# Layer 1 of a recommendation model: embeddings stationary and 512 columns of W1 moving in seven of eight blocks, the sums turned at a block's end

## The chip, the cores and the metric

One core of one Trainium2 chip. The metric is the device time of one execution in microseconds (us), the median of several. TensorE (PE) multiplies, its weight loads are listed apart as PEld; ScalarE (ACT) and VectorE (DVE) move and transform; GpSimd (POOL) issues the gathers; SyncE (SP) issues plain transfers.

## The reference, cut to what matters

```python
B, F_CAT, F_CONT, V, D = 2048, 26, 13, 12500, 64        # batch, features, vocabulary, width
H1, H2 = 1024, 512
first = sum(cat_t1[f, cat[:, f]]) + sum(cont_t1 * cont)
E = concat([cat_t2[f, cat[:, f]], cont_t2 * cont], axis=1)          # 2048 x 39 x 64
s = sum(E, axis=1);  fm_second = 0.5 * sum(s * s - sum(E * E, axis=1), axis=1)
h = relu(batchnorm(E.reshape(2048, 2496) @ W1 + b1, g1, be1))       # statistics over the batch
h = relu(batchnorm(h @ W2 + b2, g2, be2))
out = sigmoid(bias + first + fm_second + (h @ W3 + b3)[:, 0])       # returned as [1 - out, out]
```

## The kernel before, in words

The batch of 2048 is 16 tiles of 128 rows, taken two at a time in 8 blocks of 256 rows (BT = 2, BC = 256). The 26 categorical features are 13 pairs k = 0..12 (KT = 13). A pair is one 128-row slice of W1's first 1664 rows.

**Gathers.** POOL fetches each pair of each block with 4 indirect DMAs (2 tiles by 2 features, L255), 416 in all. Ahead of a pair's four it waits for `transposed`, `summed`, `squared` and `idx_ready` (L246 to L249). The first lets it run at most three pairs ahead of TensorE's transposes (five in the first block): the gather of pair k of a block waits until pair k - 3 is transposed. DVE makes the indices at the start (`find_rows`, L459) and copies those of the next block into `idx_now` pair by pair (`stage_indices`).

**Layer 1 in a block.** TensorE turns a pair (`transpose`, L735: two 128x128 transposes into one of three PSUM buffers), ACT copies it to `x_sb` (L286), and TensorE multiplies it two pairs later (LEAD = 2) with all of W1's 1024 channels: 8 products (L744), in each of which a 128x128 piece of W1 is stationary and the block's 256 rows of `x_sb` move. The trace has two records for each such fp32 product. The sums have the channels on the partitions and the batch along the columns. The continuous features add one product of 14 rows per channel chunk at the block's head (`continuous`, L787). The 8 chunks of sums fill 4 PSUM banks. `HELD` says which two chunks go into a bank: (0, 7), (1, 2), (3, 4), (5, 6).

**A block's end** (`finish`). TensorE finishes bank after bank with the last two pairs. After the second bank it does the next block's small products (`misc_products`) and transposes its pair 0, after the fourth its pair 1 (NEXT_AT). ACT copies each bank to `h1` (`sums_out`, L299), squares and copies the next block's pairs 0 and 1 in between, and DVE takes the batch statistics from `h1` (L528). `continuous` of the next block waits for `acc_free` of each bank.

**The last block** (b = 7) stands outside the loop. There the products catch up: two pairs are multiplied behind the transpose of pair 3, two behind that of pair 7, and from then on each pair is multiplied behind its own transpose. DVE takes the statistics straight from PSUM (`last_stats`, L598), makes scale and shift of layer 1 in five parts (`norm1`), ACT makes `hhi` and `hfull` (L362, L370), DVE `hlo` (L613), and layer 2 (L819) runs through to the end.

Each engine works through its list in program order. There is no scheduler. The order is the one in which the code is written.

## Time and profile before

| | us |
|---|---|
| time, median of 3 runs (lowest, highest) | 632.85 (632.6, 633.41) |
| the profiled execution, its own time | 632.65 |
| its span, first to last instruction | 630.9 |
| PE busy | 558.8 |
| PEld busy | 447.9 |
| POOL busy | 393.5 |
| ACT busy | 212.4 |
| DVE busy | 148.7 |
| mean granted clock of TensorE | 0.981 of 2.4 GHz |

The busy times are of the span. TensorE's records overlap, since matmuls are pipelined and their ends are modelled: the distance from start to start says more than a record's length. A row of the timeline merges like instructions that follow one another and gives their number.

### The profile page before, as it was taken

What the parts mean: (1) busy time and instruction counts of PE and PEld (TensorE: products, weight loads), DVE (VectorE), ACT (ScalarE), POOL (GpSimd) and SP (SyncE); (2) the same over time, 40 slices, a digit from 0 to 9 for tenths busy, and PEclk for the clock granted to TensorE, in tenths of its full rate; (3) what the DMA queues carried; (4) which work ended last, traced back from release to release, by engine and by line L of the source; (5) the groups of instructions that cost most, each with busy time, mean ns of one, the idle gap of its engine ahead of it and who ended that gap; (6) DMA issues with size and microseconds to landing.
All of it is one profiled execution on the core that took longest, in us unless ns stands there. A gap on an engine that the chain in (4) does not pass through costs nothing.

```text
span 630.9 us, 8473 instructions
## 1 busy us (share of the span) xinstructions
PE 558.8 (89%) x2534; PEld 447.9 (71%) x2534; DVE 148.7 (24%) x465; ACT 212.4 (34%) x682; POOL 393.5 (62%) x423
## 2 busy tenths in 40 slices
PE   6999898789778977799779978998799999999998
PEld 1588786568666866687658766776678877888886
DVE  1111130013001201130013101311122204754365
ACT  1223132223222322232223222322223414998575
POOL 5777777777777777777777777777777771000000
PEclk9789999999999999998999899989998999999999
DMA  8953333334332333234323432374233331000000
GB/s 256 346 137 28 27 27 27 27 26 27 27 28 25 28 27 27 27 26 28 27 26 27 28 26 27 27 161 26 27 27 28 28 27 10 1 2 0 1 0 2
DMA packets 18139, 26.79 MB, mean 42 GB/s; under 512 B 7699, under 2 KB 7947, under 8 KB 18124
## 3 DMA queue, kind: packets, MB, share of 16 engines
q0 software_dynamic: 13312, 13.87, 28.1%
q1 hardware_dynamic: 4496, 12.66, 5.7%
q8 instruction: 8, 0.13, 0.1%
q10 hardware_dynamic: 316, 0.07, 0.1%
q14 instruction: 7, 0.06, 0.0%
HBM read 26.56 MB, written 0.02 MB: 42 GB/s over the span
## 4 chain that ended last, share of the span: by engine, by line
PE 45%; DMA 31%; issue 12%; POOL 5%; ACT 2%; DVE 2%; POOLq 1%; ACTq 0%; DVEq 0%; SPq 0%
DMA emb<-in_table,idx_now 31%; PE bank L744 20%; PE bank L819 14%; POOL emb L255 5%; PE bank L787 4%; PE bank L718 2%; PE bank L735 2%; ACT junk L293 2%; DVE idx_now L477 1%; PE bank L777 1%; DMA h<-in_w 1%; DVE bank L494 0%; PE bank L778 0%; ACT h L421 0%; POOLq L137 0%
## 5 line engine op out<-in xcount | busy, mean ns | idle before, releaser
L255 POOL DMA_INDIRECT emb<-in_table,idx_now x416 | 392.8, 944 | 129.7 <-issue 115.7
L744 PE MATMUL bank<-x_sb,w_sb 128*128 128x256 f32 x1664 | 384.3, 386 | 2.4 <-ACT x_sb L286 2.4
L744 PEld LDWEIGHTS bank<-x_sb,w_sb 128*128 128x128 f32 x1664 | 314.7, 194 | 44.3 <-ACT x_sb L286 3.6
L293 ACT ACTIVATE junk<-emb 128x128 bf16<-128x128 f32 x208 | 64.2, 309 | 253.3 <-DMA emb<-in_table,idx_now 241.0
L494 DVE TENSOR_TENSOR bank<-emb,bank 128x260 f32<-128x260 f32 x91 | 39.3, 432 | 318.8 <-DMA emb<-in_table,idx_now 318.8
L735 PE MATMUL bank<-ident,emb 128*128 128x128 f32 x208 | 43.9, 294 | 59.1 <-DMA emb<-in_table,idx_now 58.2
L735 PEld LDWEIGHTS bank<-ident,emb 128*128 128x128 f32 x208 | 23.2, 141 | 88.4 <-DMA emb<-in_table,idx_now 80.2
L286 ACT ACTIVATE x_sb<-bank 128x256 f32<-128x256 f32 x104 | 38.3, 369 | 65.4 <-PE bank L735 65.3
L819 PE MATMUL bank<-hhi,w2hi 128*128 128x512 f32 x128 | 50.8, 397 | 0.0
L819 PE MATMUL bank<-hhi,w2lo 128*128 128x512 f32 x128 | 50.4, 394 | 0.0
L819 PE MATMUL bank<-hlo,w2hi 128*128 128x512 f32 x128 | 39.0, 396 | 0.3 <-DVE hlo L613 0.3
L293 ACT ACTIVATION_READ_ACCUMULATOR junk<-emb (+1 forms) x208 | 38.9, 187 | 0.0
L299 ACT ACTIVATE h<-bank 128x512 f32 (+1 forms) x32 | 19.0, 595 | 56.3 <-PE bank L744 56.3
L528 DVE BATCH_NORM_STATS2 stats<-h x56 | 21.1, 419 | 56.7 <-ACT h L299 56.7
L787 PE MATMUL bank<-cont_sb,m_sb 14*128 14x256 f32 x128 | 32.5, 407 | 0.0
L362 ACT ACTIVATE hhi<-h,bn 128x512 fp32r<-128x512 f32 x32 | 25.9, 809 | 10.0 <-PE bank L819 7.8
L613 DVE TENSOR_TENSOR hlo<-hfull,hhi 128x512 fp32r<-128x512 f32 x32 | 22.1, 690 | 30.4 <-ACT hfull L370 30.4
L787 PEld LDWEIGHTS bank<-cont_sb,m_sb 14*128 14x128 f32 x128 | 24.8, 198 | 5.5 <-issue 1.3
L819 PEld LDWEIGHTS bank<-hlo,w2hi 128*128 128x128 f32 x128 | 23.9, 187 | 6.5 <-DVE hlo L613 0.7
L819 PEld LDWEIGHTS bank<-hhi,w2hi 128*128 128x128 f32 x128 | 24.0, 187 | 6.2 <-issue 0.3
L819 PEld LDWEIGHTS bank<-hhi,w2lo 128*128 128x128 f32 x128 | 24.0, 187 | 5.7
L370 ACT ACTIVATE hfull<-h,bn 128x512 f32<-128x512 f32 x32 | 25.7, 803 | 0.0
(83 smaller groups left out, 171.6 us busy)
## 6 DMA issues: line engine op xcount, KB each, us to landing
emb<-in_table,idx_now POOLq DMA_INDIRECT x416, 3.3
w_sb<-in_w SPq DMA_DIRECT2D x13, 512.0 KB, 19.4
h<-in_w SPq DMA_DIRECT2D x6, 512.0 KB, 7.2
w2raw<-in_w SPq DMA_DIRECT2D x8, 256.0 KB, 5.4
h<-in_w SPq DMA_DIRECT2D x1, 256.0 KB, 12.7
idx_all<-in_cat SPq DMA_DIRECT2D x1, 182.0 KB, 2.5
cont_sb<-in_cont_t SPq DMA_DIRECT2D x8, 13.0 KB
diag<-in_cont_diag ACTq DMA_DIRECT2D x1, 45.5 KB, 2.1
```

What stands on the lines that cost most here:

```text
L255: nc.gpsimd.indirect_dma_start(out=emb[:, j, at:at + ROW], out_offset=None, in_=table, in_offset=bass.IndirectOffsetOnAxis(ap=idx_now[:, j ...
L286: nc.scalar.activation(x_sb[:, k, :], tp[k % TP], ACT.Copy).then_inc(x_ready, 1)
L293: nc.scalar.activation(junk[:, :], emb[:, j, k * PAIR + 1:k * PAIR + 1 + P], ACT.Square, accum_out=esq[:, ds(b * BT + j, 1), k]).then_inc( ...
L362: nc.scalar.activation(hhi[:, k, :], src, ACT.Relu, bias=bn1[:, SHIFT, k:k + 1], scale=bn1[:, SCALE, k:k + 1]).then_inc(h_high, 1)
L370: nc.scalar.activation(hfull[:, i % 2, :], h1[:, k, n * NB2:(n + 1) * NB2], ACT.Relu, bias=bn1[:, SHIFT, k:k + 1], scale=bn1[:, SCALE, k:k ...
L494: nc.vector.tensor_tensor(tot, rows, tot, ALU.add).then_inc(summed, 1)
L528: nc.vector.bn_stats(stats1[:, c, ds(b, 1), :].rearrange("p b s -> p (b s)"), h1[:, c, ds(b * BC, BC)]).then_inc(stats1_done, 1)
L613: nc.vector.tensor_tensor(hlo[:, k, :], hfull[:, i % 2, :], hhi[:, k, :].bitcast(f32), ALU.subtract).then_inc(h_split, 1)
L735: done = nc.tensor.transpose(tp[s][:, j * P:(j + 1) * P], emb[:, j, k * PAIR + 1:k * PAIR + 1 + P], ident[:, :])
L744: return nc.tensor.matmul(acc[c], w1_sb[:, k, c * P:(c + 1) * P], x_sb[:, k, :], start=False, stop=stop, skip_group_check=True)
L787: done = nc.tensor.matmul(acc[c], m_sb[:, c * P:(c + 1) * P], cont_sb[:, :], start=(c == HELD[m][0]), stop=False, skip_group_check=True)
L819: done = nc.tensor.matmul(bank2(n, m), w[:, k, cols], x[:, k, :], start=(k == 0 and i == 0), stop=(k == C1 - 1 and i == 2))
```

## The change

In blocks 0 to 6 the operands of layer 1 change places. A 128-column tile of `x_sb` (128 rows of the batch) is stationary, and 512 channels of W1 move (`tile_products`): 4 products per pair in place of 8, each into a whole bank. `sums` lists the banks as (half of the channels, tile): (0,0), (0,1), (1,0), (1,1). `continuous_tiles` is changed in the same way. The sums now have the batch on the partitions. So at a block's end ACT copies each bank to a scratch part of `h1`, the columns of the last block (`stage`); TensorE turns them with 16 transposes of 128x128 back into the four banks (`turn`); and ACT copies the banks out as before (`sums_out`), after all of the staging. Block 7 keeps its products, with chunks 2m and 2m + 1 in bank m. `HELD`, `LAST_AT` and a wait ahead of the last product go, and `last_stats` and `last_sums_out` follow the new banks. At the start DVE writes the first block's indices into `idx_all` and copies them to `idx_now` pair by pair. In the gather's waits `idx_ready` moves ahead of `summed`.

The diff, cut to its core:

```diff
@@ -136,7 +136,9 @@
     with ExitStack() as ctx:
         bank = [ctx.enter_context(nc.psum_tensor(f"bank{i}", [P, 512], f32)) for i in range(8)]
-        acc = [bank[q // 2][:, q % 2 * BC:q % 2 * BC + BC] for q in (0, *range(2, C1), 1)]
+        acc = [bank[c * BC // 512][:, c * BC % 512:c * BC % 512 + BC] for c in range(C1)]
+        HALF = H1 // 2
+        sums = [(half, j) for half in range(H1 // HALF) for j in range(BT)]
         tp = [bank[ACC_BANKS + i][:, 0:BC] for i in range(TP)]
         z = bank[4][0:TILES, 0:P]
         misc = bank[ACC_BANKS][:, BC:BC + BT * 128].rearrange("p (j c) -> p j c", j=BT)
...
@@ -196,10 +198,6 @@
         def bank2(n, m):
             return bank[(n + 1) % 2 * C2 + m][:, :]
-
-        HELD = [(0, C1 - 1)] + [(2 * m - 1, 2 * m) for m in range(1, ACC_BANKS)]
-
-        LAST_AT = [0, 1, 1, 2, 2, 3, 3, 4]
         W2_AT = {k: k - LEAD for k in range(LEAD, C1 + LEAD)}
...
@@ -244,9 +242,9 @@
                 for k in range(KT):
                     pool.wait_ge(transposed, b * KT + (KT + k + 1 - ahead))
+                    pool.wait_ge(idx_ready, b * KT + (k + 1))
                     pool.wait_ge(summed, b * KT + (k + 1))
                     pool.wait_ge(squared, b * (BT * KT) + BT * (k + 1))
-                    pool.wait_ge(idx_ready, b * KT + (k + 1))
                     pool.sem_inc(slot_open, 1)
                     for j in range(BT):
                         for half in range(2):
...
@@ -293,22 +291,26 @@
                     nc.scalar.activation(junk[:, :], emb[:, j, k * PAIR + 1:k * PAIR + 1 + P], ACT.Square,
                                          accum_out=esq[:, ds(b * BT + j, 1), k]).then_inc(squared, 1)
-            def copy_sums(b, m):
-
-                first, second = HELD[m]
-                nc.scalar.activation(h1[:, first:second + 1:second - first, ds(b * BC, BC)],
+            def stage(b, i):
+
+                half, j = sums[i]
+                act.wait_ge(sums_full, b * ACC_BANKS + (i + 1 + EMPTY))
+                chunks = h1[:, :, :].rearrange("p (q j) n -> p q j n", j=BT)[:, half * BT:(half + 1) * BT, j, :]
+                nc.scalar.activation(chunks[:, :, (BLOCKS - 1) * BC:],
+                                     bank[i][:, :].rearrange("p (q n) -> p q n", n=BC),
+                                     ACT.Copy).then_inc(staged, 1)
+
+            def sums_out(b, m):
+
+                act.wait_ge(acc_full, b * ACC_BANKS + (m + 1 + EMPTY))
+                nc.scalar.activation(h1[:, 2 * m:2 * m + 2, ds(b * BC, BC)],
                                      bank[m][:, :].rearrange("p (c n) -> p c n", n=BC),
                                      ACT.Copy).then_inc(acc_free[m], 1)
-            def sums_out(b, m):
-
-                act.wait_ge(acc_full, b * ACC_BANKS + (m + 1 + EMPTY))
-                copy_sums(b, m)
-
             def last_sums_out(m):
-                act.wait_ge(stats1_done, C1 * (BLOCKS - 1) + HELD[m][1] + 1)
-                copy_sums(BLOCKS - 1, m)
+                act.wait_ge(stats1_done, C1 * (BLOCKS - 1) + 2 * m + 2)
+                sums_out(BLOCKS - 1, m)
             def cont_squares(b):
                 act.wait_ge(cont_in, 16 * (b + 1))
...
@@ -324,11 +326,13 @@
                     x_copy(b, k)
                     if k == KT // 2:
                         cont_squares(b + 1)
+                for i in range(ACC_BANKS):
+                    stage(b, i)
+                    if i in NEXT_AT:
+                        square(b + 1, NEXT_AT[i])
+                        x_copy(b + 1, NEXT_AT[i])
                 for m in range(ACC_BANKS):
                     sums_out(b, m)
-                    if m in NEXT_AT:
-                        square(b + 1, NEXT_AT[m])
-                        x_copy(b + 1, NEXT_AT[m])
             b = BLOCKS - 1
...
@@ -386,11 +390,11 @@
             hidden_high(0, 1)
             hidden_full(0, 1)
             std1(2)
-            last_sums_out(1)
+            last_sums_out(0)
             act.wait_ge(norm1_ready, 3)
             hidden_high(0, 2)
             hidden_full(0, 2)
-            last_sums_out(2)
+            last_sums_out(1)
             std1(3)
             hidden_high(0, 3)
             hidden_full(0, 3)
...
@@ -398,10 +402,10 @@
             hidden_high(0, 4)
             hidden_full(0, 4)
             std1(4)
-            last_sums_out(3)
+            last_sums_out(2)
             hidden_high(0, 5)
             hidden_full(0, 5)
-            last_sums_out(0)
+            last_sums_out(3)
             act.wait_ge(norm1_ready, 5)
             for k in range(6, C1):
                 hidden_high(0, k)
...
@@ -456,7 +460,7 @@
             SCRATCH_KT = 4
-            def find_rows(t0, t1, to):
+            def find_rows(t0, t1):
                 cols = slice(t0 * CAT, t1 * CAT)
...
@@ -478,11 +482,13 @@
                                       src[:, ds(first_tile, BT), 2 * k:2 * k + 2]).then_inc(idx_ready, 1)
             dve.wait_ge(idx_first, 16)
-            find_rows(0, BT, idx_now[:, :, :])
-            dve.sem_inc(idx_ready, SCRATCH_KT)
+            find_rows(0, BT)
+            for k in range(SCRATCH_KT):
+                stage_indices(k, 0)
             dve.wait_ge(idx_in, 16)
-            find_rows(BT, TILES, idx_all[:, BT * CAT:TILES * CAT].rearrange("p (t f) -> p t f", f=CAT))
-            dve.sem_inc(idx_ready, KT - SCRATCH_KT)
+            find_rows(BT, TILES)
+            for k in range(SCRATCH_KT, KT):
+                stage_indices(k, 0)
             def add_up(b, k):
                 rows = emb[:, :, k * PAIR:(k + 1) * PAIR]
...
@@ -594,7 +600,7 @@
             def last_stats(c):
-                dve.wait_ge(last_full, LAST_AT[c] + 1)
+                dve.wait_ge(acc_full, b * ACC_BANKS + (c // 2 + 1 + EMPTY))
                 nc.vector.bn_stats(stats1[:, c, b, :], acc[c]).then_inc(stats1_done, 1)
             def mean1(c):
...
@@ -620,12 +626,12 @@
             last_stats(0)
             mean1(0)
+            last_stats(1)
             norm1(0)
-            last_stats(1)
             mean1(1)
             last_stats(2)
+            last_stats(3)
             norm1(1)
-            last_stats(3)
             mean1(2)
             mean1(3)
             h_low(0, 0)
...
@@ -736,10 +742,46 @@
                                                emb[:, j, k * PAIR + 1:k * PAIR + 1 + P], ident[:, :])
                 done.then_inc(transposed, 1)
+            def tile_products(k, i, stop=False):
+
+                half, j = sums[i]
+                cols, channels = slice(j * P, (j + 1) * P), slice(half * HALF, (half + 1) * HALF)
+                return nc.tensor.matmul(bank[i][:, :], x_sb[:, k, cols], w1_sb[:, k, channels], start=False,
+                                        stop=stop, skip_group_check=True)
+
             def x_wait(b, k):
                 pe.wait_ge(x_ready, x_done(b, k))
                 pe.wait_ge(w1_in[k], 16)
+            def multiply_tiles(b, k):
+                x_wait(b, k)
+                for i in range(ACC_BANKS):
+                    tile_products(k, i)
+
+            def finish(b):
+
+                for k in range(KT - LEAD, KT):
+                    x_wait(b, k)
+                for i in range(ACC_BANKS):
+                    for k in range(KT - LEAD, KT):
+                        done = tile_products(k, i, k == KT - 1)
+                    done.then_inc(sums_full, 1)
+                    if i in NEXT_AT:
+                        if NEXT_AT[i] == 0:
+                            misc_products(b + 1)
+                        transpose(b + 1, NEXT_AT[i])
+                for m in range(ACC_BANKS):
+                    turn(b, m)
+
+            def turn(b, m):
+
+                pe.wait_ge(staged, b * ACC_BANKS + (m // BT + 1) * BT)
+                for c in range(2):
+                    for j in range(BT):
+                        done = nc.tensor.transpose(bank[m][:, c * BC + j * P:c * BC + (j + 1) * P],
+                                                   h1[:, m * BT + j, (BLOCKS - 1) * BC + c * P:][:, 0:P], ident[:, :])
+                done.then_inc(acc_full, 1)
+
             def product(k, c, stop=False):
                 return nc.tensor.matmul(acc[c], w1_sb[:, k, c * P:(c + 1) * P], x_sb[:, k, :], start=False,
                                         stop=stop, skip_group_check=True)
...
@@ -747,25 +789,9 @@
             def multiply(b, k):
                 x_wait(b, k)
                 for c in range(C1):
-                    if k == KT - 1 and c == C1 - 1:
-                        pe.wait_ge(stats1_done, C1 * (BLOCKS - 1) + 1)
                     done = product(k, c, k == KT - 1)
-                    if k == KT - 1 and c in (0, 2, 4, 6, 7):
-                        done.then_inc(last_full, 1)
-
-            def finish(b):
-
-                for k in range(KT - LEAD, KT):
-                    x_wait(b, k)
-                for m in range(ACC_BANKS):
-                    for k in range(KT - LEAD, KT):
-                        for c in HELD[m]:
-                            done = product(k, c, k == KT - 1)
-                    done.then_inc(acc_full, 1)
-                    if m in NEXT_AT:
-                        if NEXT_AT[m] == 0:
-                            misc_products(b + 1)
-                        transpose(b + 1, NEXT_AT[m])
+                    if k == KT - 1 and c % 2:
+                        done.then_inc(acc_full, 1)
             def misc_products(b):
...
@@ -779,23 +805,31 @@
                                             start=True, stop=True)
                 done.then_inc(misc_full, 1)
+            def continuous_tiles(b):
+
+                for i, (half, j) in enumerate(sums):
+                    pe.wait_ge(acc_free[i], b + EMPTY)
+                    done = nc.tensor.matmul(bank[i][:, :], cont_sb[:, j * P:(j + 1) * P],
+                                            m_sb[:, half * HALF:(half + 1) * HALF], start=True, stop=False,
+                                            skip_group_check=True)
+                done.then_inc(cont_used, 1)
+
             def continuous(b):
-
-                for m in range(ACC_BANKS):
-                    pe.wait_ge(acc_free[m], b + EMPTY)
-                    for c in HELD[m]:
-                        done = nc.tensor.matmul(acc[c], m_sb[:, c * P:(c + 1) * P], cont_sb[:, :],
-                                                start=(c == HELD[m][0]), stop=False, skip_group_check=True)
+                for c in range(C1):
+                    if c % 2 == 0:
+                        pe.wait_ge(acc_free[c // 2], b + EMPTY)
+                    done = nc.tensor.matmul(acc[c], m_sb[:, c * P:(c + 1) * P], cont_sb[:, :],
+                                            start=(c % 2 == 0), stop=False, skip_group_check=True)
                 done.then_inc(cont_used, 1)
             misc_products(0)
             for k in range(LEAD):
                 transpose(0, k)
             with pe.Fori(0, BLOCKS - 1) as b:
-                continuous(b)
+                continuous_tiles(b)
                 for k in range(LEAD, KT):
                     transpose(b, k)
-                    multiply(b, k - LEAD)
+                    multiply_tiles(b, k - LEAD)
                 finish(b)
```

TensorE at a block's end, before: from the last products over pair 1's transposes (the second L735 row) and the loop's branch to the last block's head.

```order
L744 MATMUL bank<-x_sb,w_sb 128x256 x8
L733 REGISTER_ALU
L735 MATMUL bank<-ident,emb 128x128 x2
L794 REGISTER_ALU
L794 COMPARE_AND_BRANCH
L787 MATMUL bank<-cont_sb,m_sb 128x256 x8
L735 MATMUL bank<-ident,emb 128x128 x2
```

The same place on TensorE after. L781 is the turning, L749 the products with 512 columns.

```order
L749 MATMUL bank<-w_sb,x_sb 128x512 x4
L739 REGISTER_ALU
L741 MATMUL bank<-ident,emb 128x128 x2
L778 ISA
L781 MATMUL bank<-ident,h_50 128x128 x8
L778 REGISTER_ALU
L781 MATMUL bank<-ident,h_50 128x128 x8
L828 REGISTER_ALU
L828 COMPARE_AND_BRANCH
L821 MATMUL bank<-cont_sb,m_sb 128x256 x8
L741 MATMUL bank<-ident,emb 128x128 x2
```

Sixteen transposes have come between pair 1's transposes and the continuous products.

ACT at a block's end, before: the copies of banks 2 and 3 (L299), then squares (L293) and copy (L286) of the next block's pair 1.

```order
L299 ACTIVATE h_50<-bank 128x2x256
L305 REGISTER_ALU
L299 ISA
L299 ACTIVATE h_50<-bank 128x2x256
L292 REGISTER_ALU
L293 ISA
L293 ACTIVATE junk,esq<-emb 128x128
L292 REGISTER_ALU
L293 ISA
L293 ACTIVATE junk,esq<-emb 128x128
L285 REGISTER_ALU
L286 ACTIVATE x_sb<-bank 128x256
```

The same place on ACT after, from the staging of bank 3 (L299) to the copies out of banks 0 to 2 (L306).

```order
L299 ACTIVATE h_50<-bank 128x2x256
L290 REGISTER_ALU
L291 ISA
L291 ACTIVATE junk,esq<-emb 128x128
L290 REGISTER_ALU
L291 ISA
L291 ACTIVATE junk,esq<-emb 128x128
L283 REGISTER_ALU
L284 ACTIVATE x_sb<-bank 128x256
L306 ISA
L306 ACTIVATE h_50<-bank 128x2x256
L306 ISA
```

All four copies that free the banks now stand behind pair 1's squares and copy.

## Rows read from the trace of the kernel before

**Rows 1.** Timeline of POOL (start, length, engine, line, operation, count, [idle before]): the gathers.

```profile
4.82 1.14 POOL L255 DMA_INDIRECT emb<-in_table,idx_now  x1 [3.24 <-issue]
...
289.69 0.94 POOL L255 DMA_INDIRECT emb<-in_table,idx_now  x1 [0.30 <-issue]
...
494.41 0.94 POOL L255 DMA_INDIRECT emb<-in_table,idx_now  x1 [0.30 <-PE bank L735]
...
523.12 0.94 POOL L255 DMA_INDIRECT emb<-in_table,idx_now  x1 [0.30 <-issue]
```

**Rows 2.** Timeline of PE, heads of block 1 and of block 4.

```profile
88.17 0.44 PE L735 MATMUL bank<-ident,emb 128*128 128x128 f32 x2
88.45 3.62 PE L744 MATMUL bank<-x_sb,w_sb 128*128 128x256 f32 x16
...
283.12 0.44 PE L735 MATMUL bank<-ident,emb 128*128 128x128 f32 x2
283.39 5.31 PE L744 MATMUL bank<-x_sb,w_sb 128*128 128x256 f32 x16
```

**Rows 3.** Timeline of PE, head of block 7 and its run to the last gather.

```profile
473.65 0.38 PE L735 MATMUL bank<-ident,emb 128*128 128x128 f32 x2
473.97 3.71 PE L787 MATMUL bank<-cont_sb,m_sb 14*128 14x256 f32 x16
477.61 0.44 PE L735 MATMUL bank<-ident,emb 128*128 128x128 f32 x2
477.89 5.31 PE L744 MATMUL bank<-x_sb,w_sb 128*128 128x256 f32 x16
...
490.16 0.38 PE L735 MATMUL bank<-ident,emb 128*128 128x128 f32 x2
...
493.83 0.38 PE L735 MATMUL bank<-ident,emb 128*128 128x128 f32 x2
...
497.50 0.38 PE L735 MATMUL bank<-ident,emb 128*128 128x128 f32 x2
...
501.52 0.44 PE L735 MATMUL bank<-ident,emb 128*128 128x128 f32 x2 [0.18 <-DMA emb<-in_table,idx_now]
...
517.53 0.38 PE L735 MATMUL bank<-ident,emb 128*128 128x128 f32 x2
521.95 0.38 PE L735 MATMUL bank<-ident,emb 128*128 128x128 f32 x2
...
526.63 0.44 PE L735 MATMUL bank<-ident,emb 128*128 128x128 f32 x2
```

**Rows 4.** Timeline of ACT at the head of block 7.

```profile
473.95 0.60 ACT L299 ACTIVATE h<-bank 128x512 f32 x1 [1.13 <-PE bank L744]
...
475.27 0.36 ACT L286 ACTIVATE x_sb<-bank 128x256 f32<-128x256 f32 x1
```

**Rows 5.** Timeline of PE at the start of block 0.

```profile
23.32 0.66 PE L735 MATMUL bank<-ident,emb 128*128 128x128 f32 x4
...
30.85 5.60 PE L744 MATMUL bank<-x_sb,w_sb 128*128 128x256 f32 x16
```

**Rows 6.** Stretches of PE (stretch: us, PE busy, PEclk, DMA share, GB/s), the clock's falls and returns.

```profile
24.00:26.00 2.00, 2.00 (x7) 0.66 1.00 287
34.00:35.00 1.00, 1.00 (x5) 0.57 1.00 366
...
287.00:288.00 1.00, 1.00 (x5) 0.78 0.54 29
...
478.00:479.00 1.00, 1.00 (x6) 0.80 0.33 23
482.00:483.00 1.00, 1.00 (x6) 1.00 0.35 19
```

**Rows 7.** Timeline of DVE, first index copy, and the statistics behind the last products.

```profile
16.50 0.16 DVE L477 COPY idx_now<-idx_all 128x4 int32<-128x4 int32 x1
...
528.28 0.43 DVE L598 BATCH_NORM_STATS2 stats<-bank 128x6 f32<-128x256 f32 x1 [13.11 <-PE bank L744]
```

8 lines of the change are left out of this document (4 added, 4 removed).

## The prediction

> **What bounds the kernel now.** First the timeline of POOL. The gathers start at 4.82 and the last of 416 at 523.12 [rows 1]: 518.3 us in 415 steps, 1.249 us each, and nothing beyond the usual gap stands between them. A block has 52, so it takes 64.9 us. Then the timeline of TensorE. In a block it needs less: after a pair's transposes the next pair's follow 3.67 us later where it is not waiting (493.83 to 497.50 [rows 3]), and a pair's four gathers take 4.99. So TensorE waits for gathers through most of a block, and work put there costs nothing while it catches up.
>
> That isn't so in block 7. I read its row of transposes from 473.65 to 526.63 [rows 3] and look for waits. There the products also catch up two pairs (behind pair 3 and behind pair 7), and from pair 8 on each pair waits for its own copy, 4.42 us from pair to pair (517.53 to 521.95). Spare time shows in two places only: pair 7 could have started at 497.50 + 3.67 = 501.17 and started at 501.52 (0.35), pair 12 at 521.95 + 4.42 = 526.37 and started at 526.63 (0.26). From the head of block 7 to the end of layer 1 TensorE has 0.6 us to spare. Everything behind it (layer 2, the ends) is TensorE too. So I ask of the change what it does to the start of block 7.
>
> The clock is the third view. At the heads of blocks 4 and 7 the granted clock falls to the lower level, 1.2 of 2.4 GHz, and 8 products take 5.31 us; at the head of block 1 they take 3.62 and nothing falls [rows 2, 3]. One fall costs 1.69 us, so it lasts 3.4. In block 7 it begins at 478.6 (0.80 over the us from 478) and is over by 482; in block 4 it is over at 287.44 (0.78 over the us from 287) [rows 6]. It comes 4.9 us after pair 1's transposes (473.65 to 478.6), behind a stretch in which TensorE had only transposes and the 14-row products. It ends 4.0 to 4.1 us after the first product of layer 1: 30.85 to 34.86 in block 0, 283.39 to 287.44, 477.89 to 482.0 [rows 2, 3, 5, 6].
>
> **The parts, against the profiled execution, 632.65 us (span 630.9 and 1.75 around it; 0.2 under the median of 632.85).**
>
> *Start.* The first gather waited for one write of `idx_now`. Now a write of `idx_all` and one copy of 0.16 us [rows 7] stand ahead of it. POOL never stalls later, so the delay reaches the end: +0.2. The other 12 copies are ready within about 5 us; pair 1's gathers come 5 us in, pair 4's 20. The order of the four waits on POOL is worth nothing, as all were met long before.
>
> *Products, blocks 0 to 6.* 104 products of 256 columns become 52 of 512. The stream of columns is the same. A record takes (3.67 - 0.22) / 16 = 0.216 us start to start [rows 3]; 512 cycles at 2.4 GHz are 0.213, so at most 0.003 us per record can go. In a block that is 104 records, 0.3 us, hidden by the gathers. On the path lie only those behind the last gather of block 6, 24 records fewer: -0.1. Bounds: 0 and -0.1.
>
> *Turning.* 16 transposes. Four in a row took 0.66 us and two 0.38 [rows 5, 3], so 0.14 each and 2.2 in all; taken as if nothing overlapped, 0.22 each (a pair's 0.44), 3.5 in all. At the head of block 7: pair 1's transposes start at 473.65, turning from 473.9 to 476.1. The staging of bank 3 on ACT takes the place of the copy at 473.95 (0.60 [rows 4]) and is done at 474.55, when 5 of the 16 have been made and those for banks 0 and 1 still run: no wait.
>
> *The banks' release.* This is the new wait. `continuous` needs bank 0 free. Before, its copy stood early in ACT's list. Now all four copies out stand behind the staging, the squares and the copy of pair 1, which starts at 475.27 [rows 4]. The first copy out starts when that one is nearly through, about 475.55, and ends at 476.15. The others follow 0.5 us apart, and TensorE needs them 0.86 apart. So `continuous` starts at 476.2 where it started at 473.97 [rows 3]: 2.2 us late. Turning is hidden behind ACT here. If it took 3.5 it would be 3.5 late. Behind the waiting product stand pair 2's transposes and all of block 7.
>
> *The clock.* The stretch without products of layer 1 grows from 4.2 us (473.65 to 477.89) to 6.5. With the fall at 478.6 again, `continuous` would have ended at 476.2 + 3.64 = 479.84; the 1.24 us left take 2.5, pair 2's transposes start at 481.1, the products at 481.4, and with the return 4.0 later the low level lasts 6.8 us and costs 3.4, against 1.7 in this execution. Bounds: none (0), one as long as before (1.7), or one like that of block 0, from 24.64 (0.66 over 24 to 26) to 34.86, 10.2 us (5.1) [rows 6]. I take 3.4. It is worked out from the two falls nearest in kind.
> The Trainium skill (TensorE: Matmul & The Clock Gate, Part 4: PE-mode transpose) says that transposes don't count as activity for the clock. By it the 16 transposes add to the quiet stretch and don't shorten it, which is the 3.4. If they did count, the fall would be as before or absent. No row here shows transposes alone long enough to tell.
>
> *Sum for block 7.* Late by 2.2 + 3.4 - 1.7 = 3.9, less 0.6 to spare: +3.3. The gathers don't add to it: pair 7's were issued at 494.41 [rows 1] and wait for pair 4's transposes, 490.16 + 0.38 + 3.9 = 494.4, so they may lose 0.1, and TensorE is the later one by then.
>
> *The other six boundaries.* At 283.12 TensorE did pair 2's transposes, done by 283.56; the gathers of pair 5 start at 289.69 [rows 1, 2] and need them by 289.4. 2.2 and the 1.2 of slow `continuous` fit in. Pair 3's, some 5.4 us later, are needed 5.0 later and have 1.6 to spare with all of 3.9. After that TensorE gains 1.3 us a pair. Price: 0. ACT's 4 added copies of 0.6 and DVE's later statistics have the same cover: `keep_misc`, on which pair 3's transposes wait, comes at about 479, pair 3 after 483.
>
> *Behind the last product.* `last_stats(0)` waits for product 1, not 0: 528.28 [rows 7] moves by one product, 0.43. But DVE then has chunk 3's sums one product earlier, and the first `hlo`, for which layer 2 waits, stood behind chunk 3. Bounds: 0, if that wait for chunk 3 is what held it, and +0.43, if the whole list moves. I take +0.1, since the list from there on is the same.
>
> Sum: 632.65 + 0.2 - 0.1 + 3.3 + 0.1 = 636.15. I forecast **636.1 us**.
>
> **Rivals.**
> A. *The clock does not fall longer.* TensorE is kept at the upper level by the turning, or falls as before. With no fall, 2.2 - 1.7 = 0.5 is within the 0.6 to spare: 632.65 + 0.2 = 632.9. With one fall of 1.7: 2.2 - 0.6 = 1.6, 634.5. For it: the head of block 1 had no fall at all [rows 2]. Against: the quiet stretch becomes half as long again, and TensorE even idles a moment in it. Chance 0.2.
> B. *The transposes throttle the gathers at each boundary.* The longest fall, 5.1, and the slow turning (3.5 in place of 2.2) make 3.5 + 5.1 - 1.7 = 6.9, at pair 3 in place of 5.5 to spare: 1.4 lost at each of six boundaries, 8.4, beside 6.9 - 0.6 = 6.3 in block 7: up to 647; with stalls of a few tenths 638 to 640. It decides from 5.5 us late at pair 3. Against: each term would be at its bound. Chance 0.07.
> C. *Faster.* Only a shorter step of the gathers shortens blocks 0 to 6, and 364 steps lie ahead of block 7. Half as many weight loads from SBUF could do it if they disturb POOL now. It decides from 1.236 us a step in place of 1.249: 364 x 0.0125 = 4.6 less, which turns 636.15 into 631.6. Against: POOL's record is 0.94 wherever it stands, whether TensorE works beside it or waits [rows 1]. Time 631, chance 0.03.
>
> **How the numbers follow.** Forecast 0.7, A 0.2, B 0.07, C 0.03. What a measurement of this kernel can tell is about 0.2%, 1.27 us: 631.6 to 634.1 is "same". Of A a bit over half falls in it, and some of the forecast where the fall is short: same 0.17, faster 0.03, slower 0.8. Range: lower end 633.2, inside A's two cases; upper end 638.2, for a fall as long as block 0's (632.65 + 0.2 + 2.2 + 5.1 - 1.7 - 0.6 = 637.85) and a little of the slower turning.
>
> **What would show it.** In the profile after: gathers still 1.249 apart to the end of block 6, the first 0.2 later; `continuous` 2.2 us later behind pair 1 at each boundary, released by ACT's copy out (L306); the granted clock low for 6 to 7 us at the head of block 7; pair 7's transposes and all behind them in block 7 without a wait for a gather, pair 12's at about 530. Wrong would be: waits for gathers at pairs 7 and 12 of block 7 (then A), gaps in POOL's row at pairs 5 and 6 (then B), or turning at 0.22 each or more.

## The result: 1.2 us slower, 2.1 us less than forecast

| | before | after |
|---|---|---|
| median, us (14 runs each) | 632.82 | 633.98 |
| lowest, highest | 632.54, 633.72 | 632.92, 635.9 |
| the profiled execution, own time | 632.65 | 633.85 |
| its span | 630.9 | 632.1 |
| PE busy, PEld busy | 558.8, 447.9 | 571.1, 311.2 |
| mean granted clock | 0.981 | 0.973 |

The ratio is 1.0018, with an interval of 1.001 to 1.0026: the change costs 0.6 to 1.6 us. The forecast was 636.1 with a range of 633.2 to 638.2, slower with a chance of 0.8. Sign and range hold; of the size only a third came (+1.16 of +3.3). By the forecast's own band for "same", 631.6 to 634.1, the median falls in it, and that had a chance of 0.17. All ratios here are of fast runs alone, those within 1.5% of the kernel's fastest; only on the chips of 741 us and more were there others.

The times after fall into three clusters: 3 runs at 632.9 to 633.1, 8 at 633.6 to 634.3, and 3 at 635.6 to 635.9. The profiled execution is of the middle one. The last cluster will matter below.

### The profile page after: what moved, and what is told of

It is laid out like the page before. It is cut to its first block, busy times and chain, and to the rows that moved or that the text cites. A ratio compares the mean times of both kernels' runs of the same rounds, so it can differ in the third digit from the quotient of the medians.

```text
span 632.1 us, 7257 instructions
## 1 busy us (share of the span) xinstructions
PE 571.1 (90%) x1862; PEld 311.2 (49%) x1862; DVE 147.1 (23%) x478; ACT 227.1 (36%) x710; POOL 394.4 (62%) x423
## 4 chain that ended last, share of the span: by engine, by line
PE 50%; DMA 24%; issue 12%; POOL 7%; ACT 4%; DVE 1%; ACTq 1%; POOLq 0%; DVEq 0%; SPq 0%
DMA emb<-in_table,idx_now 23%; PE bank L749 18%; PE bank L853 14%; PE bank L786 8%; POOL emb L253 7%; PE bank L812 4%; PE bank L741 2%; ACT junk L291 2%; PE bank L724 2%; PE bank L803 1%; ACT h L306 1%; DMA h<-in_w 1%; PE bank L821 1%; ACT x_sb L284 1%; DVE idx_now L481 1%
## 5 line engine op out<-in xcount | busy, mean ns | idle before, releaser
L749 PE MATMUL bank<-w_sb,x_sb 128*128 128x512 f32 x728 | 337.8, 610 | 0.0
L749 PEld LDWEIGHTS bank<-w_sb,x_sb 128*128 128x128 f32 x728 | 136.1, 196 | 141.0 <-issue 141.0
L500 DVE TENSOR_TENSOR bank<-emb,bank 128x260 f32<-128x260 f32 x91 | 39.3, 431 | 292.2 <-DMA emb<-in_table,idx_now 292.1
L786 PE MATMUL bank<-x_sb,w_sb 128*128 128x256 f32 x208 | 48.9, 392 | 2.4 <-ACT x_sb L284 2.4
L786 PEld LDWEIGHTS bank<-x_sb,w_sb 128*128 128x128 f32 x208 | 39.9, 196 | 8.8 <-ACT x_sb L284 3.6
L534 DVE BATCH_NORM_STATS2 stats<-h x56 | 19.6, 411 | 86.6 <-ACT h L306 86.6
L299 ACT ACTIVATE h<-bank 128x512 f32<-128x512 f32 x28 | 16.7, 597 | 55.1 <-PE bank L749 55.1
L812 PE MATMUL bank<-m_sb,cont_sb 14*128 14x512 f32 x56 | 29.4, 668 | 1.8 <-ACT h L306 1.8
```

The source lines that it names most:

```text
L500: nc.vector.tensor_tensor(tot, rows, tot, ALU.add).then_inc(summed, 1)
L534: nc.vector.bn_stats(stats1[:, c, ds(b, 1), :].rearrange("p b s -> p (b s)"), h1[:, c, ds(b * BC, BC)]).then_inc(stats1_done, 1)
L749: return nc.tensor.matmul(bank[i][:, :], x_sb[:, k, cols], w1_sb[:, k, channels], start=False, stop=stop, skip_group_check=True)
L786: return nc.tensor.matmul(acc[c], w1_sb[:, k, c * P:(c + 1) * P], x_sb[:, k, :], start=False, stop=stop, skip_group_check=True)
L812: done = nc.tensor.matmul(bank[i][:, :], cont_sb[:, j * P:(j + 1) * P], m_sb[:, half * HALF:(half + 1) * HALF], start=True, stop=False, sk ...
```

## The profile after

Half of the weight loads went, as the changed operands say, and the time didn't follow. The costliest groups of the profile's page (busy us, mean ns of one, idle before):

```profile
L749 PE MATMUL bank<-w_sb,x_sb 128*128 128x512 f32 x728 | 337.8, 610 | 0.0
L749 PEld LDWEIGHTS bank<-w_sb,x_sb 128*128 128x128 f32 x728 | 136.1, 196 | 141.0 <-issue 141.0
```

728 loads do what 1456 did in blocks 0 to 6. A load lay beside the product ahead of it before and does so now, so no product starts earlier: a pair's four products take 3.60 us (8 records), as eight took 3.62.

The timeline of PE at the heads of blocks 1 and 7, to be laid beside [rows 2, 3]:

```profile
84.25 1.91 PE L781 MATMUL bank<-ident,h 128*128 128x128 f32 x16
86.46 3.69 PE L812 MATMUL bank<-m_sb,cont_sb 14*128 14x512 f32 x8 [0.30 <-ACT h L306]
90.08 0.44 PE L741 MATMUL bank<-ident,emb 128*128 128x128 f32 x2
90.36 5.29 PE L749 MATMUL bank<-w_sb,x_sb 128*128 128x512 f32 x8
...
473.36 0.38 PE L741 MATMUL bank<-ident,emb 128*128 128x128 f32 x2
473.57 1.91 PE L781 MATMUL bank<-ident,h 128*128 128x128 f32 x16
475.78 3.72 PE L821 MATMUL bank<-cont_sb,m_sb 14*128 14x256 f32 x16 [0.30 <-ACT h L306]
479.43 0.44 PE L741 MATMUL bank<-ident,emb 128*128 128x128 f32 x2
479.70 5.31 PE L786 MATMUL bank<-x_sb,w_sb 128*128 128x256 f32 x16
...
499.32 0.38 PE L741 MATMUL bank<-ident,emb 128*128 128x128 f32 x2
503.00 0.38 PE L741 MATMUL bank<-ident,emb 128*128 128x128 f32 x2
...
523.36 0.38 PE L741 MATMUL bank<-ident,emb 128*128 128x128 f32 x2
527.78 0.44 PE L741 MATMUL bank<-ident,emb 128*128 128x128 f32 x2
```

From pair 1's transposes to the continuous product it is 2.42 us (473.36 to 475.78), before 0.32 [rows 3]: 2.10 more. The wait that ends last is ACT's copy out (L306), with TensorE idle for 0.30. The row of pair 7 (503.00) follows pair 6's by 3.68 and has no wait, and pair 12's (527.78) follows by 4.42 with none. The 0.35 and 0.26 that TensorE waited for gathers before are used up.

The timeline of ACT at the same place, to be laid beside [rows 4]:

```profile
473.56 0.60 ACT L299 ACTIVATE h<-bank 128x512 f32<-128x512 f32 x1 [1.12 <-PE bank L749]
...
475.14 2.05 ACT L306 ACTIVATE h<-bank 128x512 f32 x4
```

On ACT come staging, squares, pair 1's copy, and only then the four copies out. The first of these lets TensorE go, 0.30 behind the end of the turning at 475.48. So two paths of nearly the same length run side by side here: 1.91 us of turning on TensorE itself, and ACT's list. The wait shows ACT's alone, but without it the turning would still take most of the 2.10 (experiment 7).

The clock, in stretches of PE (stretch, PE busy, PEclk, DMA share, GB/s), to be laid beside [rows 6]:

```profile
90.00:91.00 1.00, 1.00 (x5) 0.94 0.35 25
94.00:95.00 1.00, 1.00 (x3) 0.86 0.51 35
...
479.00:480.00 1.00, 1.00 (x7) 0.99 0.38 27
480.00:481.00 1.00, 1.00 (x4) 0.50 0.35 27
483.00:484.00 1.00, 1.00 (x6) 0.80 0.28 21
```

The low level (1.2 GHz) lasts from 479.98 to 483.4, 3.4 us, and again makes 5.31 us of the first 8 products: 1.69 lost, as before. It begins 4.2 us after the first continuous product (475.78), where it began 4.6 after it before (473.97 to 478.6). All seven heads now have such a fall (here block 1's, from 90.9 to 94.3), of the same length; before it was four of seven. Six of them stand beside gathers and cost nothing (experiment 1).

The sum for this execution: 2.10 for the banks, less 0.29 (pair 1's transposes came at 473.36, before at 473.65), is 1.81 at pair 2 (479.43 against 477.61); less 0.66 of spare time (0.34 at pair 7, 0.26 at pair 12, and 0.07 between them), 1.15 at pair 12 (527.78 against 526.63). From there to the end it is 104.32 against 104.27. 1.15 + 0.05 = 1.20, the whole difference of the two own times (633.85 - 632.65).

**A second thing, which the forecast did not see.** Timeline of POOL after, to be laid beside [rows 1]:

```profile
4.77 1.14 POOL L253 DMA_INDIRECT emb<-in_table,idx_now  x1 [3.19 <-DVE idx_now L481]
...
481.81 1.26 POOL L253 DMA_INDIRECT emb<-in_table,idx_now  x1 [0.30 <-issue]
...
487.12 1.31 POOL L253 DMA_INDIRECT emb<-in_table,idx_now  x1 [0.30 <-issue]
...
516.20 1.20 POOL L253 DMA_INDIRECT emb<-in_table,idx_now  x1 [0.30 <-issue]
...
523.94 0.95 POOL L253 DMA_INDIRECT emb<-in_table,idx_now  x1 [0.30 <-issue]
```

And of DVE:

```profile
481.56 0.69 DVE L568 TENSOR_TENSOR w2lo<-w2raw,w2hi 128x512 fp32r<-128x512 f32 x1 [1.46 <-ACT w2hi L346]
...
486.92 0.69 DVE L568 TENSOR_TENSOR w2lo<-w2raw,w2hi 128x512 fp32r<-128x512 f32 x1 [4.32 <-ACT w2hi L346]
...
515.89 0.69 DVE L568 TENSOR_TENSOR w2lo<-w2raw,w2hi 128x512 fp32r<-128x512 f32 x1 [3.72 <-ACT w2hi L346]
```

Three gathers of block 7 take 1.20 to 1.31 us where its others take 0.94 or 0.95. Each was issued 0.20 to 0.31 after the start of one of the eight subtractions that split W2 (L568), and each ends 0.82 after that subtraction: 481.56 + 0.69 + 0.82 = 483.07 = 481.81 + 1.26, and so on. These three put 0.94 on the row. At block 7's first gather the row had stood 0.11 ahead of before's (459.33 against 459.44), and so the last gather is issued at 523.94 and not at 523.12. Before, pair 12 started 3.51 us after the last gather's issue (523.12 to 526.63 [rows 1, 3]), waiting for it. By the same distance gathers would have let it go at 527.45 here (an estimate), 0.33 ahead of TensorE's 527.78. TensorE is the later one, by little.

## The experiments

Two sets of chips must be kept apart. The first comparison and the first four kernels below ran on chips where the kernel before takes 633 us. On the others it takes 741 to 751: TensorE, ACT and DVE stand still together for 3 to 7.4 us, 6 to 12 times in an execution (in one trace from 476.3 to 482.8), and never for so long in the six traces of the first set. What they wait for I could not settle. Their ratios are not ratios of the 633 us kernel; their rows can still be read.

**1. Which boundary costs.** Block 6 in the old form, so that only the boundary into block 7 loses staging and turning:

```diff
-            with pe.Fori(0, BLOCKS - 1) as b:
+            with pe.Fori(0, BLOCKS - 2) as b:
                 continuous_tiles(b)
                 ...
+            b = BLOCKS - 2
+            continuous(b)
+            for k in range(LEAD, KT):
+                transpose(b, k)
+                multiply(b, k - LEAD)
+            finish_old(b)
```

> The changed kernel, but block 6 has the kernel before's form too (256 rows moving, no staging, no turning): only the boundary into block 7 is undone, five of six others keep the turning. Theory 1 (only the head of block 7 counts, the others are hidden behind the gathers): the time is that of the kernel before, 632.6 to 633.0. Rival (each turning costs a seventh): 634.0 less 0.2, 633.8.

Measured: 633.47 (11 runs, 632.7 to 633.85) against 633.0, ratio 1.0004, interval 0.9995 to 1.0013. Timeline of PE, head of block 1 and then block 7:

```profile
84.36 1.91 PE L792 MATMUL bank<-ident,h 128*128 128x128 f32 x16
86.57 4.43 PE L837 MATMUL bank<-m_sb,cont_sb 14*128 14x512 f32 x8 [0.30 <-ACT h L306]
...
91.41 6.00 PE L760 MATMUL bank<-w_sb,x_sb 128*128 128x512 f32 x8
...
501.77 0.44 PE L752 MATMUL bank<-ident,emb 128*128 128x128 f32 x2 [0.51 <-DMA emb<-in_table,idx_now]
```

In this execution the clock was low for 6.8 us at the heads of blocks 1 to 6 (4.43 and 6.00 in place of 3.69 and 3.60), twice as long as in any boundary of the profile after, and the time is about that of before. The time alone doesn't decide: its interval reaches to 633.8, where the rival has it. The rows do: the gathers keep their 1.249 us a step to the end of block 6, and pair 7 waits for them again. So the six early boundaries are hidden even with a long fall, and rival B is out. The slowdown sits in the boundary into block 7.

**2. The rest of the change alone.** Old form in all blocks; the banks' order, the start, DVE's list and the waits as changed:

```diff
-                continuous_tiles(b)
+                continuous(b)
                 for k in range(LEAD, KT):
                     transpose(b, k)
-                    multiply_tiles(b, k - LEAD)
-                finish(b)
+                    multiply(b, k - LEAD)
+                finish_old(b)
```

> All blocks in the old form, with the rest of the change left: index copies at the start, the new order of the gather's waits, chunks 2m and 2m + 1 in bank m, the new order of the statistics behind the last product. I predicted +0.2 for the start and +0.1 for the end: 633.1. The trace of the changed kernel speaks for nothing at the start (first gather 0.05 earlier) and 0.05 to 0.1 at the end: 632.9. Rival: the rest makes up part of the 1.2 us, 633.3 or more.

Measured: 633.07 (11 runs, 632.71 to 634.34), ratio 1.0001, interval 0.9992 to 1.001. The first gather starts at 4.81 (before 4.82), pair 12 at 526.97. The start, the moved statistics and the order of POOL's waits cost nothing that shows, at most 0.6 us by the interval.

**3. What makes the clock fall.** The kernel before, with the continuous product padded by zeros from 14 to 128 rows (POOL and DVE write the zeros at the start; those lines are left out here):

```diff
-    m_sb = place("m_sb", [CROWS, H1], f32)
-    cont_sb = place("cont_sb", [CROWS, BC], f32)
+    m_sb = place("m_sb", [P, H1], f32)
+    cont_sb = place("cont_sb", [P, BC], f32)
```

> The kernel before with its continuous products filled up with zeros to 128 rows. Theory 2: no fall of the clock at any block head, where four of seven had one. Theory 1: no gain in time all the same, as the last gather sets the end of layer 1 with 0.6 us to spare after a fall: 632.8, and TensorE's slack in block 7 is 2.3 us in place of 0.6. Rival (falls reach the end in the kernel before too): 0.5 us or more faster.

Measured: 633.7 (11 runs, 633.02 to 635.39), ratio 1.0008, interval 0.9999 to 1.0017. No head has a fall any more; the mean granted clock is 0.995. Over all 11 executions it is 0.986 to 1.000, where 35 of the kernel before, on the same chip, have 0.949 to 0.992. Timeline of PE:

```profile
473.98 3.62 PE L792 MATMUL bank<-cont_sb,m_sb 128*128 128x256 f32 x16
477.65 3.62 PE L749 MATMUL bank<-x_sb,w_sb 128*128 128x256 f32 x16
...
497.39 0.44 PE L740 MATMUL bank<-ident,emb 128*128 128x128 f32 x2 [0.91 <-DMA emb<-in_table,idx_now]
...
527.70 0.44 PE L740 MATMUL bank<-ident,emb 128*128 128x128 f32 x2 [0.20 <-DMA emb<-in_table,idx_now]
```

So the 14-row products are what lets the clock fall at a head: TensorE is busy through them in both kernels, for as long, and only the rows differ. They are not the only thing that does. Within block 6 one fall is left (418.9 to 422.3), behind 2.11 us in which TensorE stood idle, and the trace of experiment 2 has three within blocks, behind waits for gathers of 1.89 to 2.08 us. No time is won: the median is 0.7 us above that of before, with an interval that just holds no difference. TensorE saves 1.69 us and waits for gathers instead (0.91 at pair 6, 1.22 at pair 7), even at pair 12, since here two gathers met a subtraction and the very first took 1.39 in place of 1.14. The first of the two (POOL, then DVE; the other took 1.25):

```profile
479.63 1.38 POOL L257 DMA_INDIRECT emb<-in_table,idx_now  x1 [0.30 <-issue]
```

```profile
479.51 0.69 DVE L567 TENSOR_TENSOR w2lo<-w2raw,w2hi 128x512 fp32r<-128x512 f32 x1 [2.30 <-ACT w2hi L345]
```

**4. The delay by itself.** The kernel before, with 20 more transposes of pair 1 ahead of each block's continuous product, about 2 us, and nothing else of the change:

```diff
-                for j in range(BT):
+                for j in [0, 1] * (11 if k == 1 else 1):
```

> The kernel before, with pair 1's two transposes repeated so that 20 more stand ahead of the continuous products in each block, 0.11 us each, about 2.1 us; the operands, the staging and ACT's order are those of before. Theory 1 (a delay of 2.1 us at the head of block 7 is the whole cost): 632.8 + 2.1 - 0.6 = 634.3 with a fall in block 7 and 632.8 without, so about that of the changed kernel, 634.0, with T12 of block 7 at 527.8 to 528.2. Rival (a delay is hidden by the gathers and the cost is in the changed products): 632.8.

Measured: 634.17 (12 runs, 633.13 to 635.74), ratio 1.002, interval 1.0011 to 1.0029: the changed kernel's ratio. A delay of 2 us ahead of the continuous product is enough for the whole effect. Its times cluster as after's do: 2 at 633.1 to 633.4, 5 at 633.9 to 634.2, 5 at 635.55 to 635.74. The profiled execution is one of the last. Timeline of PE:

```profile
473.49 2.57 PE L735 MATMUL bank<-ident,emb 128*128 128x128 f32 x22
475.98 4.17 PE L787 MATMUL bank<-cont_sb,m_sb 14*128 14x256 f32 x16
480.09 0.69 PE L735 MATMUL bank<-ident,emb 128*128 128x128 f32 x2
...
493.80 0.38 PE L735 MATMUL bank<-ident,emb 128*128 128x128 f32 x2
...
529.61 0.38 PE L735 MATMUL bank<-ident,emb 128*128 128x128 f32 x2
```

And its stretches:

```profile
479.00:480.00 1.00, 1.00 (x4) 0.55 0.43 31
...
485.00:486.00 1.00, 1.00 (x4) 0.54 0.33 21
```

Here the fall begins 3.1 us after the continuous product and lasts from 479.1 to 485.9, 6.8 us. It costs 0.46 in that product, 0.25 in pair 2's transposes and 2.65 behind them, 3.36 in all; pair 4 stands 3.64 later than before (493.80 against 490.16) and pair 12 2.98 later. These are the forecast's terms: 2.01 late where it had 2.2, 3.36 for the fall where it had 3.4, and 2.98 at pair 12 where it had 3.3. By its time this is the case in 5 of 12 executions here. A long fall would put the changed kernel at 633.85 + 1.7 = 635.55 (an estimate), and 3 of its 14 executions lie at 635.6 to 635.9. I have no profile of one of those three. Nor is there one of the 3 at 632.9 to 633.1, which would fit a block 7 without a fall (2.10 - 0.29 - 1.69 = 0.12, within the spare time).

The fall of block 7 doesn't simply move with the products. Here they come 2.0 us later than before (475.98 against 473.97) and the fall begins at 479.1, 0.5 later. It begins at 478.6 in the traces of before and of experiment 1, at 478.1 in that of experiment 2 and at 480.0 in that of the changed kernel.

**5. Do transposes count for the clock?** On the other chips: the change with each turning done three times over, 48 transposes in a row; and the change without staging and turning, which leaves layer 1's sums of blocks 0 to 6 in the wrong layout.

```diff
-                for c in range(2):
+                for c in [0, 1] * 3:
                     for j in range(BT):
```

> Each of the 16 turning transposes is made three times, into the same place, so 48 a block, about 5.7 us in place of 1.9. Theory 1a (transposes keep TensorE's clock at the upper level; only the 14-row continuous products are quiet): the clock stays high through all 48 and falls, if it falls, about 4.2 to 4.6 us after the continuous products start, as now; these start 3.5 us later than in the changed kernel (479.3 against 475.8), block 7 is TensorE's, and the time is 634.0 + 3.5 = 637.5, with some tenths for gathers that now wait. Rival 1b (transposes are quiet, as I predicted): the clock falls inside the 48 transposes, they take up to twice as long, and the time is 641 or more.

> The changed kernel without the turning and the staging: ACT copies the banks straight to h1 and frees them where the kernel before does (so h1 holds the sums with the batch on the partitions). What is left is the exchange of the operands alone, the index copies and the new banks. Theory 1 (the cost is the late release of the banks at the head of block 7): the continuous products start about 0.3 us behind pair 1's transposes again, block 7 waits for gathers at pairs 7 and 12 again, and the time is that of the kernel before, 632.6 to 633.0. Rival (512-column products, or the index copies, cost something themselves): it stays near 634.

The repeats, on a second and a third chip, were to find one of the speed of the first comparison:

> Each turning transpose three times, 48 a block, as before. Theory 1a (transposes hold the clock up): full clock over the 48, a fall only 3.3 to 4.6 us after the continuous products start; these start 3.5 later than in the changed kernel; 634.0 + 3.5 = 637.5. Rival 1b (transposes are quiet): a fall inside the 48, 641 or more.

> Each turning transpose three times, 48 a block. Theory 1a (transposes hold the clock up): full clock over the 48, a fall only 3 to 5 us after the continuous products start; these start 3.5 later than in the changed kernel; 637.5. Rival 1b (transposes are quiet): a fall inside the 48, 641 or more.

> The changed kernel without turning and staging, as before (h1 holds the sums with the batch on the partitions), for the first run fell on a chip where every kernel took 18% longer. Theory 1: 632.8 to 633.1, block 7 waits for gathers at pairs 7 and 12. Rival (the 512-column products or the rest cost): near 634.

> The changed kernel without turning and staging (h1 holds the sums with the batch on the partitions). Theory 1: 632.8 to 633.1, block 7 waits for gathers at pairs 7 and 12. Rival (the 512-column products or the rest cost): near 634.

Turning three times was run three times: 771.07, 768.3 and 771.77, ratios 1.0243, 1.0184 and 1.0175 (each within 0.007). Without turning: 736.22, 734.85 and 731.95, ratios 0.9828, 0.9797 and 0.9816 (each within 0.0042). Timeline of PE in the third run of the first, where no pause broke the row, and its stretches:

```profile
350.25 5.40 PE L781 MATMUL bank<-ident,h 128*128 128x128 f32 x48
355.59 1.39 PE L812 MATMUL bank<-m_sb,cont_sb 14*128 14x512 f32 x2
```

```profile
354.00:355.00 1.00, 1.00 (x12) 1.00 0.36 25
...
358.00:359.00 1.00, 0.50 (x1) 0.50 0.41 23
```

48 transposes run 0.11 us apart at the full clock, and it is down by 358, behind the first 14-row products and a pause of TensorE. Five heads in the three traces have all 48 in a row in 5.40 us, and none has a fall among them, while behind the start of 14-row products a fall came after 2.2 to 4.8 us. So transposes hold the clock up. By the Trainium skill (TensorE: Matmul & The Clock Gate, Part 4: PE-mode transpose) they don't count as activity; these rows disagree, and the measurement decides for transposes of this kind (fp32, 128x128, back to back).

The times tell that on those chips the boundaries are on the path. I take it that TensorE comes late out of the pauses and has nothing to catch up in; that is not shown. The 32 further transposes of seven boundaries are 224 x 0.11 = 25 us, and by the ratios they cost 11 to 18 against the kernel of experiment 6. So there the turning is paid at several of the seven boundaries, and not at the last alone as on the first chips. Without it the changed products are even 13 to 16 us faster than the kernel before on those chips; why was not settled, and it was not run on the first. (Its rows show the boundary without turning: where no pause breaks it, the continuous product starts 0.31 behind pair 1's transposes, as before.)

**6. The changed kernel with 128 rows.** The edit of experiment 3 on the kernel after; run four times on those chips (751.67, 754.0, 752.59, 751.52).

> The changed kernel with both operands of the continuous products filled up with zeros from 14 to 128 rows; the result is the same, and the columns and the number of products too. Theory 2 (the clock falls because these products use 14 of 128 rows): the granted clock stays 1.00 at all seven block heads, 8 products take 3.6 there and not 5.3, block 7's pair 7 comes 1.7 us earlier, and the time is 634.0 less 1.2 or so, 632.8 to 633.0, since the gathers take over as the bound after 1.15 us. Rival (zeros count as little as missing rows, or the fall hangs on something else in that stretch): falls as now, 634.0.

> The changed kernel with the continuous products filled up with zeros to 128 rows, as before. In the kernel before the same edit left no fall at any of seven heads. Theory 2: none here either, block 7's pair 7 comes 1.7 us earlier than with one fall, and the time is 633.0, with a spread as small as the kernel before has it, since the two sizes of the fall (1.7 and 3.4) are what spreads the changed kernel from 632.9 to 635.9. Rival: 634.0 and the same spread.

> The changed kernel with the continuous products filled up with zeros to 128 rows. Theory 2: no fall at any block head, pair 7 of block 7 comes 1.7 us earlier than with one fall, 633.0, and a spread as small as that of the kernel before. Rival: 634.0 and the spread of the changed kernel (632.9 to 635.9).

> The changed kernel with the continuous products filled up with zeros to 128 rows. Theory 2: no fall at any block head, 633.0, and a spread as small as that of the kernel before. Rival: 634.0 and the spread of the changed kernel (632.9 to 635.9).

Against the kernel before the ratios are 1.0009, 1.0024, 1.0029 and 1.0072, with intervals from 0.9976 to 1.0107; the last alone is clear of 1. A stretch behind a pause, timeline of PE:

```profile
104.97 1.97 PE L786 MATMUL bank<-ident,h 128*128 128x128 f32 x8 [9.11 <-ACT h L302]
106.73 5.52 PE L817 MATMUL bank<-m_sb,cont_sb 128*128 128x512 f32 x8
...
112.31 3.60 PE L754 MATMUL bank<-w_sb,x_sb 128*128 128x512 f32 x8
```

The clock, down from 100.4 on in a pause of 9.11 us, is back at 110.6, inside the padded product, and the first products of layer 1 take 3.60: zeros in the rows were enough to bring it back. What the padding brings the changed kernel in time on the first chip was not measured.

**7. ACT's copies out first.** Pair 1's squares and copy moved behind the copies out, to take away the wait for L306:

```diff
-                    if i in NEXT_AT:
-                        square(b + 1, NEXT_AT[i])
-                        x_copy(b + 1, NEXT_AT[i])
+                    if i == 1:
+                        square(b + 1, 0)
+                        x_copy(b + 1, 0)
                 for m in range(ACC_BANKS):
                     sums_out(b, m)
+                square(b + 1, 1)
+                x_copy(b + 1, 1)
```

> ACT copies the turned banks out ahead of pair 1's squares and copy, not behind them. Theory 1: the banks are free as soon as they are turned, continuous starts at 475.5 (the end of 16 transposes) in place of 475.78, and block 7 and the end come 0.3 us earlier: 633.7. So the turning itself (1.9 us) is as long as ACT's path, and undoing ACT's order gives back a seventh of the delay. Rival (ACT's order is the cause, the turning is hidden): 2 us earlier up to the gathers' bound, 632.8.

> ACT copies the turned banks out ahead of pair 1's squares and copy, as before. Theory 1: continuous starts 0.3 us earlier behind pair 1's transposes (2.1 in place of 2.4), as the 1.9 us of turning are nearly as long as ACT's path; 633.7. Rival (ACT's order is the cause): 2 us earlier, 632.8 to 633.0.

Measured on the other chips: 760.35 and 760.77, ratios 1.0115 (1.0062 to 1.0169) and 1.0111 (1.007 to 1.0152). It was then combined with experiment 6:

> The changed kernel with both edits: ACT copies the turned banks out ahead of pair 1's squares and copy, and the continuous products are filled up with zeros to 128 rows. Theory: continuous starts 2.1 us behind pair 1's transposes (1.9 us of turning) in place of 2.4, no fall at any head, block 7 waits for its last gathers again, and the time is that of the kernel before, 632.8 to 633.0. Rival (something else in the change costs): 633.5 or more. On a chip with ACT's pauses the time says little, and the rows of the trace are what counts.

Measured: 748.88 (6 runs) against 746.18, ratio 1.0002 (0.9949 to 1.0055). It gains nothing there in time. What the order of ACT's list is worth stands in the rows. Timeline of PE in the first trace of this experiment, at a boundary where no pause comes before the continuous product:

```profile
264.68 0.38 PE L743 MATMUL bank<-ident,emb 128*128 128x128 f32 x2
264.90 1.91 PE L783 MATMUL bank<-ident,h 128*128 128x128 f32 x16
266.74 2.84 PE L814 MATMUL bank<-m_sb,cont_sb 14*128 14x512 f32 x6
```

The continuous product follows the turning without a wait, 2.06 us behind pair 1's transposes (264.68 to 266.74) in place of 2.43. The second trace has 2.06 as well (347.45 to 349.51), and the combined kernel has 1.97 at the head of block 7 (570.60 to 572.57). So of the 2.10 us ACT's order makes at most 0.4; the rest is TensorE's own turning. On the first chips the edit was not run; by these rows it could win back 0.4 us at most (an estimate).

**8. The subtractions off DVE.** The kernel before, with the eight subtractions of W2 on POOL behind its last gather. It was the candidate to beat both:

```diff
+            for i in range(C1):
+                pool.wait_ge(w2hi_ready, i + 1)
+                nc.gpsimd.tensor_tensor(w2lo[:, i, :], w2raw[:, i, :], w2hi[:, i, :].bitcast(f32),
+                                        ALU.subtract).then_inc(w2_ready, 1)
```

> The kernel before with the eight w2lo subtractions of block 7 moved from DVE (where they run beside the gathers) to POOL's list behind its last gather. Theory 3 (a gather that is issued during such a subtraction waits for its end, 0.26 to 0.37 us each time, and whether one does is chance, since it hangs on TensorE's beat): no gather beside the first over 1.0 us, the last issued at 523.1 in every execution, and the time at the lower edge of the kernel before, 632.6, with the spread of 632.5 to 633.8 gone; against a median of 633.0 of the kernel before in the last comparison 0.3 us less. It is the version that could beat both. Rival (the long gathers come from elsewhere): long gathers stay, 633.0. A danger: POOL's subtractions take longer than DVE's 0.69 and share its way to SBUF, so that hlo or w2lo comes late behind 531; then 0.5 us or more slower.

Measured, on another chip of the second set: 739.83 (12 runs, 737.36 to 745.25) against 741.42, ratio 0.9994, interval 0.9965 to 1.0023. Timeline of POOL:

```profile
628.46 0.94 POOL L255 DMA_INDIRECT emb<-in_table,idx_now  x1 [0.30 <-issue]
629.42 9.83 POOL L265 TENSOR_TENSOR w2lo<-w2raw,w2hi 128x512 fp32r<-128x512 f32 x8
```

Behind the first gather one took 1.02, at 553.27, and no other more than 0.96. It too was issued during an operation with two SBUF operands, of another line (timeline of DVE):

```profile
553.18 0.29 DVE L520 TENSOR_TENSOR ssum_sq<-ssum 128x128 f32<-128x128 f32 x1
```

553.18 + 0.29 + 0.82 = 554.29 = 553.27 + 1.02.
POOL needs 1.23 us for each subtraction in place of DVE's 0.69. Those 8 are over at 639.25; layer 2's first product starts at 641.15. So it can be done, and it takes the collisions with W2's subtractions away; that it gains is not shown, since an interval of 0.6% of 740 us says nothing on 0.3 us.

## Why the prediction was right in sign and wrong in size

- **What bounds the kernel: right.** Gathers to the end of block 6, TensorE from the head of block 7. Experiment 1 shows the six hidden boundaries, experiment 4 the one that isn't.
- **Turning: right in length, wrong in place.** 1.91 us for 16, forecast 2.2. "Turning is hidden behind ACT here" is true of the wait alone: the two paths are of nearly the same length, and with ACT's out of the way 2.06 of the 2.43 us behind pair 1's transposes are still there (experiment 7). The sum doesn't suffer, since it takes the longer of the two.
- **The banks' release: right.** 2.2 forecast, 2.10 measured, released by L306.
- **The clock: the term that was mis-sized, and the step that failed.** It was "With the fall at 478.6 again, `continuous` would have ended at ..., the low level lasts 6.8 us and costs 3.4". It fixed the fall to one place, took the transposes for part of the quiet stretch, and so made a long fall the usual case. The transposes hold the clock up (experiment 5), and what lets it fall at a head are the 14-row products, which take as long as before (experiment 3). In the profiled execution, one of the eight of the middle cluster, the fall began at 479.98, was 3.4 us long again and cost 1.69, as before: the net of this term is 0 and not +1.7. The sum with it is 2.2 + 0 - 0.6 = 1.6, which is rival A's second case (634.5), with a chance of 0.2; the first comparison's profile came out at 633.85. The long fall of the forecast exists (experiment 4, 3.36 us) and by the times comes in a minority of the executions. What decides between a short and a long one stays open. The forecast's return, 4.0 us after the first product of layer 1, was no rule: it is 3.7 in the trace after (479.70 to 483.40) and 5.4 in that of experiment 4 (480.57 to 485.93).
- **The start: wrong by a little.** +0.2 forecast, -0.05 measured (4.77 against 4.82); experiment 2 has 4.81. The head of block 7 came 0.29 earlier as well, of which the start and the -0.1 for the products of block 6 would explain about half; the rest has no cause that was shown. Against the forecast the two own times leave 2.30 us (636.15 - 633.85): the clock 1.7, the start 0.25, the rest of the earlier head 0.14, and 0.05 to 0.1 each for the release, the spare time and the end.
- **Spare time: right.** 0.6 forecast, 0.66 used.
- **Behind the last product: right.** +0.1 forecast, +0.05 measured, with the first statistics 0.43 later behind pair 12 (529.86 - 527.78 against 528.28 - 526.63).
- **Not seen: the gathers that meet a subtraction.** The forecast said that gathers add nothing. In this execution they alone would have put pair 12 at about 527.45, so a change that had cost TensorE nothing would still have looked up to 0.8 us slower in such an execution. Which of the eight subtractions meet a gather changes between executions; in the trace of before none did to any cost. That fits with the spread of 1.2 us in the kernel before, but no slower execution of it was profiled.
- **Rival C** had nothing for it: with half of the weight loads gone, a gather's step stayed at 1.249 us to the end of block 6.

## What to carry to other kernels

Weight loads that lie beside products cost nothing here: halving them gained nothing, and what the other orientation needs to bring its result back (staging, turning, banks freed later) is paid wherever the same engine is the late one, here once in seven boundaries on a chip without pauses. When two engines' paths end within a few tenths of each other, the wait names the later one, and taking that one away wins only the few tenths: price both. When a forecast depends on a clock fall, ask of several executions where it begins, how long it lasts and how often, and carry the cases with their shares through the sum in place of fixing one. And where the time hangs on a queue that never idles, look at the neighbours of every instruction of that queue that is longer than its kin.
